# GpSimd instead of VectorE makes the row numbers of the indexed stores, two columns ahead of each two stores

## The reference, cut to what matters

```
h    = relu(layernorm(x)) @ W_in2f.T
Wij  = (smu(edge_attr_20 @ W_f1.T + b_f1) @ W_f2.T + b_f2) * edge_weight
x_ij = h[dst] * Wij                              # one row of 128 per edge
agg  = segment_sum(x_ij, src, 12500)
x    = x + smu(agg @ W_o1.T + b_o1) @ W_o2.T + b_o2
```

## Time and profile before

| what | value |
|---|---|
| timed runs (3) | 4130.75 us median, 4130.41 to 4132.45 |
| profiled execution, span from first to last instruction | 5828.1 us |
| busy in the profiled execution | PE 4390.8 us, DVE 3425.3 us, ACT 2120.4 us, POOL 3041.4 us |
| mean granted clock of TensorE in it | 0.825 of full speed |
| indexed stores | 3125, busy 3000.2 us |
| row numbers on VectorE | 784, busy 125.5 us |

### The profile page before, as it was taken

The page is one execution under the profiler, slowest core; times in us unless marked ns, Lnnn a source line. Parts: engine busy times, 40 slices in busy tenths (PEclk is TensorE's granted clock), DMA queues, the critical chain, the costliest instruction groups (busy, mean ns, idle before and its releaser), DMA issues.

```text
span 5828.1 us, 115538 instructions
## 1 busy us (share of the span) xinstructions
PE 4390.8 (75%) x32406; PEld 3600.8 (62%) x32406; DVE 3425.3 (59%) x11901; ACT 2120.4 (36%) x7301; POOL 3041.4 (52%) x3173
## 2 busy tenths in 40 slices
PE   5566557777777777777777777777778788778888
PEld 4455446666666666666666666666666666666667
DVE  6555455555565555555555555555656666566667
ACT  3455333333333333333333333333333333333332
POOL 4555555555555555555555555555555555555552
PEclk8777778787888888888788888888888888888899
DMA  5354334444443433433333333333444444445547
GB/s 163 105 134 136 111 109 130 132 130 130 131 122 108 116 112 112 115 115 112 110 113 112 117 112 112 112 111 115 129 132 133 136 141 138 136 135 146 153 143 198
DMA packets 460270, 736.98 MB, mean 126 GB/s; under 512 B 87920, under 2 KB 256218, under 8 KB 459856
## 3 DMA queue, kind: packets, MB, share of 16 engines
q1 hardware_dynamic: 292358, 461.45, 29.9%
q0 software_dynamic: 100000, 206.60, 10.6%
q10 hardware_dynamic: 67626, 65.48, 3.4%
HBM read 465.36 MB, written 267.82 MB: 126 GB/s over the span
## 4 chain that ended last, share of the span: by engine, by line
another core or an unknown queue 34%; PE 32%; issue 14%; DVE 9%; ACT 8%; ACTq 2%; DMA 1%; DVEq 1%; SPq 0%; POOL 0%
PE p_seg L1184 8%; PE p_w L1139 7%; PE p_z L1133 7%; PE p_h L1150 6%; ACT hg L691 3%; DVE product L950 2%; DVE onehot L935 1%; DVE seg_hot L976 1%; PE p_pos L1156 1%; DVE act L926 1%; ACT p_w L705 1%; PE p_pos L1172 1%; ACT gelu L680 1%; ACTq L656 1%
## 5 line engine op out<-in xcount | busy, mean ns | idle before, releaser
L558 POOL DMA_INDIRECT sorted_rows<-msg,row_idx x3125 | 3000.2, 960 | 2697.4 <-DVE msg L943 1799.2
L691 ACT ACTIVATE hg<-p_h,weight 128x128 f32<-128x128 f32 x3136 | 897.2, 370 | 3175.2 <-remote 2840.0
L1184 PEld LDWEIGHTS p_seg<-seg_hot,seg 128*128 128x128 f32 x8288 | 1241.2, 217 | 841.2 <-issue 838.4
L950 DVE CUSTOM_DVE_ANT_0 product<-onehot,p_pos,start_at 128x112 bf16<-128x112 bf16 x3136 | 848.0, 326 | 1456.2 <-remote 1426.4
L1184 PE MATMUL p_seg<-seg_hot,seg 128*128 128x112 f32 x8288 | 1316.4, 303 | 372.8 <-issue 343.1
L1139 PE MATMUL p_w<-w_f,act 128*128 128x128 f32 x6272 | 1155.1, 328 | 250.3 <-issue 245.0
L1139 PEld LDWEIGHTS p_w<-w_f,act 128*128 128x128 f32 x6272 | 989.1, 233 | 265.4 <-issue 263.8
L1133 PE MATMUL p_z<-attr,w_f 128*128 128x512 f32 x1568 | 991.9, 709 | 203.9 <-issue 109.1
L1150 PE MATMUL p_h<-win,pick 128*128 128x128 bf16 x9408 | 836.3, 251 | 284.8 <-ACT hg L691 229.9
L943 DVE TENSOR_TENSOR msg<-p_w,hg 128x512 f32<-128x512 f32 x784 | 540.6, 690 | 717.1 <-ACT hg L691 492.1
L1150 PEld LDWEIGHTS p_h<-win,pick 128*128 128x128 bf16 x9408 | 707.1, 115 | 317.7 <-issue 316.9
(11 more groups left out here) (113 smaller groups left out, 1698.4 us busy)
## 6 DMA issues: line engine op xcount, KB each, us to landing
seg<-sorted_rows SPq DMA_DIRECT2D x560, 322.5 KB
ends<-ends SPq DMA_DIRECT2D x392, 256.0 KB
seg<-sorted_rows SPq DMA_DIRECT2D x112, 516.0 KB
sorted_rows<-msg,row_idx POOLq DMA_INDIRECT x3125
sorted_rows<-zero_rows ACTq DMA_DIRECT2D x336, 129.0 KB
win<-h SPq DMA_DIRECT2D x392, 96.0 KB
attr<-in_attrT SPq DMA_DIRECT2D x392, 80.0 KB
seg<-sorted_rows SPq DMA_DIRECT2D x56, 387.0 KB
```

The source lines that it names most:

```text
L558: pool.indirect_dma_start(out=sorted_rows[:, :], out_offset=bass.IndirectOffsetOnAxis(ap=row_idx[:, slot, k:k + 1], axis=0), in_=msg[:, sl ...
L691: last = act.activation(hg[:, v, k, :], p_h[:, k, :], ACT.Copy, scale=weight[:, bass.ds(n.value(TILES_U, k), 1)])
L950: last = dve.tensor_tensor_reduce(out=product[:, k, :], in0=onehot[:, slot, k, :], in1=p_pos[:, 0:BUCKETS], scale=1.0, scalar=start_at[:, ...
L1184: last = pe.matmul(out, seg[:, it.slot, l * it.tiles + k, 0:F], seg_hot[:, it.slot, l * it.tiles + k, :], start=(k == 0), stop=(k == it.ti ...
```

## The change

The four row numbers of a unit are made by GpSimd in its own queue: two instructions of one column each, a wait for their completion, the two stores that use them, and the same again for the second pair of columns. VectorE's `row_numbers` is gone. GpSimd now waits for `s_limit` and `s_place` where it waited for `s_idx`. `s_idx` counts halves: `limits` waits for the second half of the unit four before, and `places` of unit n for the second half of unit n-2, as before by unit.

```diff
+HALVES = 2
+HALF = TILES_U // HALVES
...
-            def scatter(n, slot, tiles=TILES_U):
-                wait_for(pool, s_idx, n, 1, 1)
+            def scatter(n, v, slot, tiles=TILES_U):
+                wait_for(pool, s_limit, n, 1, 1)
+                wait_for(pool, s_place, n, 1, 1)
                 wait_for(pool, s_key, n, 1, 1)
                 wait_for(pool, s_msg, n, 1, 1)
                 pool.sem_inc(s_go, 1)
-                for k in range(tiles):
-                    pool.indirect_dma_start(out=sorted_rows[:, :],
-                                            out_offset=bass.IndirectOffsetOnAxis(ap=row_idx[:, slot, k:k + 1], axis=0),
-                                            in_=msg[:, slot, k, :], in_offset=None).then_inc(s_scat[slot], 16)
+                for h in range(HALVES):
+                    for k in range(h * HALF, (h + 1) * HALF):
+                        last = pool.tensor_scalar(row_idx[:, slot, k:k + 1], place[:, v, k:k + 1], place_max[:, slot, k:k + 1], None, ALU.min)
+                    last.then_inc(s_idx, 1)
+                    wait_for(pool, s_idx, n, HALVES, h + 1)
+                    pool.sem_inc(s_go, 1)
+                    for k in range(h * HALF, min((h + 1) * HALF, tiles)):
+                        pool.indirect_dma_start(out=sorted_rows[:, :],
+                                                out_offset=bass.IndirectOffsetOnAxis(ap=row_idx[:, slot, k:k + 1], axis=0),
+                                                in_=msg[:, slot, k, :], in_offset=None).then_inc(s_scat[slot], 16)
...
             def limits(n, slot, rnd):
-                wait_for(act, s_idx, n, 1, 1 - RING)
+                wait_for(act, s_idx, n, HALVES, HALVES * (1 - RING))
...
             def places(n, v, slot, half):
                 wait_for(dve, s_rank, n, 1, 1)
-                wait_for(dve, s_idx, n, 1, -1)
+                wait_for(dve, s_idx, n, HALVES, -HALVES)
...
-            def row_numbers(n, v, slot):
-                wait_for(dve, s_place, n, 1, 1)
-                wait_for(dve, s_scat[slot], n.over(RING), 16 * TILES_U)
-                dve.tensor_tensor(row_idx[:, slot, :], place[:, v, :], place_max[:, slot, :], ALU.min).then_inc(s_idx, 1)
...
                 if st.has(1):
-                    row_numbers(st.at(1), st.v(1), st.ring(1))
                     message(st.at(1), st.v(1), st.ring(1))
```

More of the change, by code:

```diff
@@ L571, in step @@
                     n = st.at(1)
-                    scatter(n, st.ring(1), TILES_U if n.i is not None else max(0, min(TILES_U, real_tiles - n.base * TILES_U)))
+                    scatter(n, st.v(1), st.ring(1), TILES_U if n.i is not None else max(0, min(TILES_U, real_tiles - n.base * TILES_U)))
             def add_bias(g, turn):
```

## The result

| kernel | runs | median us | lowest to highest |
|---|---|---|---|
| before | 4 | 4131.3 | 4130.41 to 4132.45 |
| changed | 4 | 6065.81 | 6063.88 to 6066.36 |

The ratio is 1.4681, 95% interval 1.4663 to 1.4699: the change makes the kernel 1935 us slower. A second set on one chip, 4 runs of the changed kernel and 19 of the kernel before, gave 6064.81 against 4131.63, ratio 1.4675 (1.4651 to 1.4700). The forecast was 5660, range 4950 to 6200.

A forecast was written before the change was run, and what follows sets the result against it. The prediction took GpSimd issuing its stores as the bound. Each half adds 0.10 + 0.27 + 0.91 - 0.30 = 0.98 us, times 1563 is 1532 us, on 4130.75: forecast 5660 us, range 4950 to 6200.

The forecast's parts named there:

- rival B: TensorE's clock joins in as it pauses more and may bind the pace: 5950 to 6450 us, chance 0.12.
- the lock: VectorE's L930 could hold up a GpSimd column by 0.38 us, 298 us if every time; not added, kept in range.
- The bound: GpSimd issuing its stores, 1.263 us each, 5.05 us a unit, binds the timed kernel; sum 4111 us against 4130.75.
- The 1697 us that were put down to the profiled execution: Profiled 5828.1 us against timed 4130.75; the surplus, perhaps in VectorE's and ScalarE's waits, was taken to belong to profiling.
- The gap before the first column: On GpSimd, from the end of a store to the first column: 0.10 us a half, bounds 0 and 0.30.
- The pair of columns: Two 128 x 1 columns on GpSimd: 0.27 us a half, bounds 0.13 (memsets) and 0.53 (selects).
- The wait and the store behind it: GpSimd waits for its own columns, then starts the store: 0.91 us a half, lower bound 0.16.
- rival A: The wake-up after GpSimd's wait on itself is cheap, 0.16 us or half hidden: 4450 to 5000 us, chance 0.14.
- The 0.30 us given back: The 0.30 us that the store had before it already, subtracted from each half's added time.
- `place` freed later: VectorE's run-ahead of GpSimd falls from four units to one to two; nothing is late, worth 0.
- Rival C: GpSimd isn't the bound, the 0.30 us between stores being there only while profiled: down to 4005 us, chance 0.06.

The follow-up runs named there:

- `more_records`: Kernel before, with SyncE counting up a semaphore 30 more times for each two units: 4136.63 us against 4131.63, ratio 1.0009.
- `one_cast`: Changed kernel with one converting instruction of four columns, smaller-of left out, one wait a unit: 5625.12 us; kernel before 5908.07, ratio 0.9523.
- `four_groups`: Changed kernel with each column ahead of its own store, four waits a unit: 7185.89 us, ratio 1.2180 to the kernel before.
- `unit_ahead_cols`: Changed kernel with the columns of unit n+1 made between the second and third store of unit n: 5263.82 us; kernel before 5908.07, ratio 0.8911.
- `after_again`: The changed kernel again, unchanged, beside the kernel before on one chip: 6064.81 us against 4131.63, ratio 1.4675.
- `one_group`: Changed kernel with all four columns ahead of the four stores, one wait a unit: 5519.46 us, ratio 0.9358 to the kernel before.

## Why the prediction was right, and where its sum was off

The mechanism was right, the size partly lucky. The measured 6065.81 us lie in the stated range, but 96 us above the forecast's own 5250 to 5970 and inside the band of rival B, 5950 to 6450, whose mechanism the traces refute. The upper part of the range was kept for B and for the lock. The kernel lost 1935 us where 1532 were forecast. (B's upper end, 6450, follows from no sum shown; the upper bounds of the forecast's terms give 4131 + 2251 = 6382.)

**The bound.** Right, and the step that carried all else. The base had GpSimd's stores end to end, 4111 us, against what the busy shares say. The trace of `more_records` shows just that, and with TensorE relieved by 249 us the time stays.

**The 1697 us that were put down to the profiled execution.** Wrong in its reason. I inferred that the surplus belonged to the recording. All 19 runs of the kernel before in the last set have a span and clock recorded (0.962 to 0.973) and took 4128 to 4138 us; those on three other chips have them too (0.818 to 0.832) and took 5806 to 5923. So the surplus goes with the chip or its state. The conclusion drawn, that the sum be made against GpSimd's bare pace, held for the runs that the result is made of. On a chip with stops the same base would have been wrong.

**The gap before the first column.** Forecast 0.10, measured 0.03 (0.04 in the median). Right in kind.

**The pair of columns.** This term of the sum was mis-sized: 0.27 us, measured 0.54. One column lasts 0.30 and the next starts 0.27 behind it. That is 0.01 above the forecast's upper bound, the two selects of 128 x 128, and not near the memset or iota. The selects are 128 times as wide and take as long, and `one_cast` converts four columns in 0.20 us: width hardly enters in these rows. What made the selects the better row was, it seems, that they read a tile; memset and iota only write. That reason is argued, not shown.

**The wait and the store behind it.** Forecast 0.91, measured 0.82: right, and rival A (0.16) is out. `four_groups`, with 3077 such waits at 0.82 us each, and `unit_ahead_cols`, where the same wait is met ahead of time and costs nothing, tell it from the columns.

**The 0.30 us given back.** Right.

**A term that was missing.** The first store behind a column takes 1.05 us and not 0.96, with a wait or without: 0.09 a half. By luck it makes up for the 0.09 by which the wait was forecast too long; the columns are what is left, 0.27 us a half, less the 0.07 of the gap.

Summed with the measured terms: 0.03 + 0.54 + 0.82 + 0.09 - 0.30 = 1.18 us a half, 1563 x 1.18 = 1844, and 4131 + 1844 = 5975 us. The columns are 0.54 x 1563 = 844 us of it and the waits 0.64 x 1563 = 1000. The remaining 91 us lie in the mean distance of the units, 7.56 against 7.42. Two things make them up.

**The lock.** Some 43 of those 91 us. Of the 3136 columns 295 took more than 0.35 us, and 292 of these overlap a tensor_scalar of VectorE. One such pair, on both engines:

```profile
2505.81 0.34 DVE L939 TENSOR_SCALAR pick<-ends,win_row 128x512 bf16<-128x512 uint16 x1
```

GpSimd's pair at 2505.78 takes 0.70 us, 0.16 more than its neighbours, and L939 ends at 2506.15. So the trace agrees with the Trainium skill (SBUF — State Buffer, "Who interferes with whom") that one waits for the other. It was GpSimd each time that could be read: L939 keeps its 0.34 us in the median. The price was 43 us and not the 298 of every time: of the 748 columns that overlap a tensor_scalar of VectorE 456 took no more than 0.35 us.

**A pause every 26 units.** The other 48 us. In 29 places the second store of a half starts 1.96 us after the first has ended and not 0.30, each time 104 stores after the place before:

```profile
2415.53 1.05 POOL L567 DMA_INDIRECT sorted_rows<-msg,row_idx  x1 [0.81 <-POOL row_idx L562]
2418.54 0.96 POOL L567 DMA_INDIRECT sorted_rows<-msg,row_idx  x1 [1.96 <-issue]
```

29 x 1.66 us is 48 us. `after_again` and `one_group` have the same 29 pauses behind the same stores, and `more_records` has none of them. What they are isn't known.

**`place` freed later.** Right that GpSimd is never late for it: its waits for `msg` ahead of a column are 35.5 us, nearly all before the first unit. VectorE waits 1563.6 us for GpSimd instead, which costs nothing.

**TensorE's clock, rival B.** The granted clock was 0.97 for the kernel before and 0.87 for the changed one on one chip. Between 1900 and 2900 us TensorE was busy 866 us at 0.98 in `more_records`, and 661 us at 0.88 in the changed kernel. But GpSimd went on without waiting for the others, so it cost nothing here. **Rival C** is out: the 0.30 us between stores are there at 4132.8 us too.

## What to carry to other kernels

Before moving work to an engine, add up the distances from start to start in its queue, not its busy share: 4 x 1.263 us a unit of 5.27 was a full queue that the page showed as 52% busy in the profiled execution, and as 74% where the kernel took 4133 us (`more_records`). An engine that waits for its own small result pays the empty queue, here 0.64 us each time, more than for the two instructions that it waited for; make such a result a step earlier (`unit_ahead_cols`), or on the engine with room. And measure a change beside the kernel that it is compared with, on the same chip.

## What the runs showed of the hardware

The stops weren't expected. In the profiled execution of the kernel before, about every second unit, VectorE and ScalarE stand idle: between 60 us and the tail VectorE 271 times for over 4 us (5.7 in the median), ScalarE 367 times (8.0). In `more_records`, on the chip without stops, it is 3 and 25 times. In the one below they and SyncE start again within 0.4 us of each other; often it is 1 to 2 us. TensorE issues in pieces meanwhile, and GpSimd works on until its queue is empty. One of them:

```profile
2796.76 0.27 PE L1139 MATMUL p_w<-w_f,act 128*128 128x128 f32 x1 [1.02 <-issue]
...
2798.54 0.95 POOL L558 DMA_INDIRECT sorted_rows<-msg,row_idx  x1 [0.30 <-issue]
2799.63 0.29 PEld L1133 LDWEIGHTS p_z<-attr,w_f 128*128 128x128 f32 x1 [1.26 <-issue]
...
2801.11 0.33 DVE L950 CUSTOM_DVE_ANT_0 product<-onehot,p_pos,start_at 128x112 bf16<-128x112 bf16 x1 [5.94 <-remote]
...
2801.42 0.89 ACT L691 ACTIVATE hg<-p_h,weight 128x128 f32<-128x128 f32 x3 [7.86 <-remote]
2801.43 0.33 SPq L460 DMA_DIRECT2D win<-h  x1
```

The results that they wait for are older: TensorE's last product for `p_h` ended at 2795.02, and ScalarE takes it at 2801.42. What stops them stays open. The number of instructions recorded isn't shown to matter, nor that it doesn't; no run on a chip with stops tested it. Whether the changed kernel would have stops on such a chip wasn't run either.
